# A sparse-attention kernel: GpSimd takes over the test for missed rows and one subtraction, and VectorE's pick moves into its guess update

## The chip, the cores and the metric

The kernel runs on one core of one Trainium2 chip. The metric is the device time of one launch in microseconds. The kernel before took 3318.77 us, the median of 3 runs (3317.39 to 3321.68). Engines are called by the profile's names: PE is TensorE, DVE is VectorE, ACT is ScalarE, POOL is GpSimd, SP is SyncE.

## The reference

The input x is 16 batches of 512 tokens of width 128. One transformer layer is computed on it:

```
x = x + layernorm(attention(layernorm(x)))
x = x + layernorm(ffn(layernorm(x)))

attention, 16 heads of width 64, 16 memory keys in front of the 512 keys:
  dots = (q @ k^T) * scale                     # per head
  dots = einsum('bhij,hk->bkij', dots, pre_proj)   # heads mixed
  dots = where(causal, -max, dots)
  vk   = top_k(dots, 64)[..., -1:]             # the 64th largest of each row
  attn = softmax(where(dots < vk, -max, dots))
  attn = einsum('bhij,hk->bkij', attn, post_proj)
  out  = (attn @ v) @ Wo + bo
ffn: down( silu(gate(x)) * up(x) ), hidden width 384
```

The costly part is the 64th largest of each of 16 x 16 x 512 rows of up to 528 scores.

## The kernel before, in words

**Tiling.** The unit of work is one mixed head of one batch: 512 query rows as four tiles of 128 rows (`t` = 0 to 3), with row lengths 144, 272, 400 and 528 (causal keys and 16 memory keys). There are 16 x 16 = 256 heads, and the program is a software pipeline of steps. Step `s` of batch `b` (`g = 16 b + s`) starts head `g` and works on several older heads at once. Batch 0 (`first`), 14 batches in a loop (`mid`, two a turn), the last batch (`last`) and a `drain` are the same code with different stages left out. Every engine has its own list of instructions, written out by hand; semaphores alone order them against each other, and nothing is reordered.

**Finding the 64th largest.** The kernel guesses a threshold for each row. ACT counts how many scores lie above the guess (the `signs` instructions, three guesses for three heads a step), and DVE moves the guess by a secant step: the *guess update*, eleven small instructions from `miss` to `guesses`, on tiles of 12 or 24 columns (L1113 to L1148). After the third move DVE counts exactly how many scores lie at or above the last guess (`count_found`, L1075, tile `found`) and masks them. POOL subtracts those scores out (L1357, `work`, four instructions a step: the *hide*), and two steps later DVE takes the eight largest of what is left with four MAX8 (L1089). Which of those nine candidates is the 64th is known from `found`. POOL makes rank minus 64 plus `found` for nine ranks (`offset`, L1338), and DVE turns that into zeros and one candidate (L1092) and sums it (L1097): the *pick*, which gives `kth`.

**Missed rows.** Where `found` is too far from the aim, the nine candidates don't hold the 64th. DVE tests that in two small instructions (`spread` L1104 and `missed` L1109). PE adds the marks of all rows up with a tiny matmul into a spare part of a score bank (`raise_flag`, L749), DVE copies the sums out (`flags`, L1072, between two score tiles), reads the total into a register and branches to an exact search (`general_kth`) for the tiles that need it.

**After the threshold.** DVE makes the masked exponentials (`probs`, L1190, four instructions) and their reciprocal sums (`rinv`, L1195). POOL waits for `rinv`, makes four diagonal matrices (`diag`, L1349), and PE uses them to transpose and scale `probs` (L784); ACT copies the result out (L926) and PE multiplies it with the values (L771).

**The order of DVE in a step**: MAX8 x4, pick, miss test, guess update, `count_found` of the two longest tiles, in steps 11 to 13 two products of the FFN (`f_up`, L1164 and L1170) between those two, `probs` x4, `rinv`, `count_found` of the two shorter tiles, then four passes over the new scores in PSUM (L1209) with the flag copy before the last of them. In steps 0, 7, 8 and 14 the statistics of a layer norm follow, in step 10 a maximum over the memory scores.

**The order of POOL in a step**: `negmax` (L1317), seed copy (L1323), memory copy (L1332), `offset` (L1338), in some steps the body of a layer norm (L1258 to L1277), `diag` x4, hide x4, `pmem` (L1363).

## Time and profile before

| | |
|---|---|
| median of the runs | 3318.77 us |
| the profiled execution | 3324.22 us, of which span 3322.4 us |
| mean granted TensorE clock | 0.954 |
| DVE busy | 2884.4 us, 87% |
| ACT busy | 2882.6 us, 87% |
| PE busy | 2794.6 us, 84% |
| POOL busy | 1737.9 us, 52% |
| DMA | mean 7 GB/s |

The span runs from the first to the last instruction of the program. Busy is time in which an engine has an instruction at work; waits, register work and branches of its sequencer are not in it. On DVE a good part of what is not busy lies in gaps of 0.03 to 0.2 us between small instructions that depend on each other. A row of the profile can hide a wait inside an instruction's duration: where an instruction was issued but could not run, its row is longer than that of its fellows.

### The profile page before, as it was taken

What the parts mean: (1) busy time and instruction counts of PE and PEld (TensorE: products, weight loads), DVE (VectorE), ACT (ScalarE), POOL (GpSimd) and SP (SyncE); (2) the same over time, 40 slices, a digit from 0 to 9 for tenths busy, and PEclk for the clock granted to TensorE, in tenths of its full rate; (3) what the DMA queues carried; (4) which work ended last, traced back from release to release, by engine and by line L of the source; (5) the groups of instructions that cost most, each with busy time, mean ns of one, the idle gap of its engine ahead of it and who ended that gap; (6) DMA issues with size and microseconds to landing.
All of it is one profiled execution on the core that took longest, in us unless ns stands there. A gap on an engine that the chain in (4) does not pass through costs nothing. (4 is left out here: it accounts for less than half of the span.)

```text
span 3322.4 us, 76028 instructions
## 1 busy us (share of the span) xinstructions
PE 2794.6 (84%) x16314; PEld 2046.5 (62%) x16314; DVE 2884.4 (87%) x12547; ACT 2882.6 (87%) x8666; POOL 1737.9 (52%) x3623
## 2 busy tenths in 40 slices
PE   6888888888878888888898878888788898888865
PEld 3466666666656666666666656666566666666654
DVE  4599888989989899998889989989889889998884
ACT  1699899998978989899898979989899898989972
POOL 3355555555545555555555545545555555555543
PEclk9999999999989999999999989999999999999987
DMA  1000000000000000000000000000000000000000
GB/s 45 7 2 2 5 8 5 9 2 5 9 5 9 2 12 2 5 9 5 9 2 12 2 5 8 2 12 2 5 9 5 9 2 12 2 5 9 2 8 4
DMA packets 31421, 22.93 MB, mean 7 GB/s; under 512 B 3201, under 2 KB 30338, under 8 KB 30722
## 3 DMA queue, kind: packets, MB, share of 16 engines
q1 hardware_dynamic: 30722, 16.03, 1.7%
q14 instruction: 555, 4.55, 0.5%
q8 instruction: 144, 2.36, 0.3%
HBM read 11.83 MB, written 4.19 MB: 5 GB/s over the span
## 5 line engine op out<-in xcount | busy, mean ns | idle before, releaser
L915 ACT ACTIVATE signs<-scores,state 128x528 int8<-128x528 f32 (+3 forms) x3072 | 1726.3, 585 | 40.5 <-DVE state L1148 40.0
L784 PE MATMUL t_bank<-diag,probs 128*128 128x128 f32 x5120 | 760.9, 308 | 453.8 <-POOL diag L1349 400.5
L1349 POOL TENSOR_SCALAR diag<-ident,rinv 128x128 f32<-128x128 f32 x1024 | 362.2, 374 | 1360.1 <-DVE rinv L1195 1360.1
L784 PEld LDWEIGHTS t_bank<-diag,probs 128*128 128x128 f32 x5120 | 694.2, 216 | 494.1 <-issue 359.1
L1357 POOL TENSOR_TENSOR work<-scores,work 128x528 f32<-128x528 f32 (+3 forms) x1024 | 889.0, 903 | 10.8 <-DVE work L1075 10.8
L760 PE MATMUL s_bank<-xn,gT 128*128 128x512 f32 (+3 forms) x2048 | 685.7, 457 | 0.9 <-ACT gT L846 0.7
L771 PEld LDWEIGHTS y_bank<-u_all,probsT 128*128 128x128 f32 x5120 | 609.0, 192 | 107.3 <-issue 98.9
L915 ACT ACTIVATION_READ_ACCUMULATOR signs<-scores,state 128x1 f32 x3072 | 646.5, 210 | 0.0
L926 ACT COPY probsT<-t_bank 128x512 f32<-128x512 f32 (+1 forms) x768 | 406.9, 530 | 266.3 <-PE t_bank L784 265.1
L771 PE MATMUL y_bank<-u_all,probsT 128*128 128x128 f32 x5120 | 617.3, 276 | 5.3 <-ACT probsT L926 5.3
L1075 DVE TENSOR_SCALAR_CACHE_REDUCE work<-scores,state 128x528 f32<-128x528 f32 (+3 forms) x1024 | 531.1, 553 | 46.2 <-DVE state L1148 46.2
L936 ACT ACTIVATE expo<-scores,negmax 128x528 f32<-128x528 f32 (+3 forms) x1024 | 546.7, 599 | 0.0
L1190 DVE SCALAR_TENSOR_TENSOR probs<-scores,kth,expo 128x528 f32<-128x528 f32 (+3 forms) x1024 | 525.5, 569 | 12.3 <-ACT expo L936 5.8
L1209 DVE TENSOR_SCALAR_CACHE_REDUCE scores<-s_bank,memmax 128x512 f32<-128x512 f32 (+3 forms) x1024 | 516.7, 543 | 6.0 <-PE s_bank L762 6.0
L760 PEld LDWEIGHTS s_bank<-xn,gT 128*128 128x128 f32 x2048 | 326.5, 193 | 227.9 <-issue 220.5
L1089 DVE MAX8 state<-work 128x8 f32<-128x528 f32 (+3 forms) x1024 | 441.6, 491 | 0.2 <-issue 0.2
L632 PE MATMUL misc<-b_all,xn 128*128 128x512 f32 x512 | 273.4, 616 | 7.5 <-ACT u_all L846 7.5
L669 PE MATMUL misc<-xn,a_all 128*128 128x512 f32 x512 | 262.5, 594 | 0.0
L762 PE MATMUL s_bank<-causal,ident 128*128 128x128 bf16 x1024 | 224.6, 219 | 0.0
L762 PEld LDWEIGHTS s_bank<-causal,ident 128*128 128x128 bf16 x1024 | 101.1, 99 | 103.3 <-issue 63.2
L846 ACT COPY u_all<-misc 128x512 f32<-128x512 f32 x256 | 151.4, 591 | 7.0 <-PE misc L632 7.0
L846 ACT COPY gT<-misc 128x512 f32<-128x512 f32 x256 | 154.2, 602 | 0.9 <-PE misc L669 0.9
(156 smaller groups left out, 2846.5 us busy)
## 6 DMA issues: line engine op xcount, KB each, us to landing
xwork<-in_L_attn_x_dram SPq DMA_DIRECT2D x17, 256.0 KB, 2.8
xres<-in_L_attn_x_dram SPq DMA_DIRECT2D x16, 256.0 KB, 2.9
out_dram<-ybuf SPq DMA_DIRECT2D x16, 256.0 KB, 2.4
u_all<-in_L_attn_Wq_dram SPq DMA_DIRECT2D x1, 512.0 KB, 3.6
u_all<-in_L_attn_Wk_dram SPq DMA_DIRECT2D x1, 512.0 KB, 4.5
u_all<-in_L_attn_Wv_dram SPq DMA_DIRECT2D x1, 512.0 KB, 5.5
u_all<-in_L_attn_Wo_dram SPq DMA_DIRECT2D x1, 512.0 KB
expo<-in_L_ffn_w_gate_dram SPq DMA_DIRECT2D x1, 192.0 KB, 4.7
```

Source lines behind the costliest of these rows:

```text
L760: nc.tensor.matmul(score_part(t, 0, KEYS[t]), lhsT=gT[s % 2][:, t * P:(t + 1) * P], rhs=xn[par][:, 0:KEYS[t]], start=True, stop=False, ski ...
L771: mm = nc.tensor.matmul(y_bank[:, t * P:(t + 1) * P], lhsT=probsT[:, h % 2, at:at + P], rhs=u_all[:, j, h * D:(h + 1) * D], start=False, s ...
L784: mm = nc.tensor.matmul(t_bank[q % 2][:, at:at + P], lhsT=probs[:, h % 2, KEY_AT[t] + j * P:KEY_AT[t] + (j + 1) * P], rhs=diag[:, t, :], s ...
L915: nc.scalar.activation(signs[:, k, AT[t]:AT[t] + ROW[t]], row(scores, ring(head_of(s, k + 1), RING), t), ACT.Sign, bias=guesses(s % STATES ...
L926: nc.scalar.copy(probsT[:, h % 2, PART_AT[q]:PART_AT[q + 1]], t_bank[q % 2][:, 0:PART_AT[q + 1] - PART_AT[q]]).then_inc(t_taken, 1)
L936: nc.scalar.activation(row(expo, ring(head_of(s, LAG_E), ERING), t), row(scores, ring(head_of(s, LAG_E), RING), t), ACT.Exp, bias=negmax[: ...
L1075: v.tensor_scalar(work[:, s % 2, AT[t]:AT[t] + ROW[t]], row(scores, slot_k, t), guessed[:, t:t + 1], None, ALU.is_ge, ALU.add, accum_out=f ...
L1089: v.max(candidates(past)[:, t, 1:9], work[:, s % 2, AT[t]:AT[t] + ROW[t]]).then_inc(select_step, 1)
L1190: v.scalar_tensor_tensor(out=probs[:, slot_p % 2, AT[t]:AT[t] + ROW[t]], in0=row(scores, slot_p, t), scalar=kth[:, bass.ds(slot_p, 1), t], ...
L1209: v.tensor_scalar(keys(scores, slot, t), score_part(t, 0, KEYS[t]), 1.0, memmax[par][:, t, bass.ds(s, 1)], ALU.mult, ALU.max, accum_out=ro ...
L1349: nc.gpsimd.tensor_scalar(diag[:, t, :], ident[:, :], rinv[:, slot_p, t:t + 1], 1.0, ALU.mult, ALU.mult).then_inc(scaled, 1)
L1357: nc.gpsimd.tensor_tensor(wrk, row(scores, slot_k, t), wrk, ALU.subtract).then_inc(hidden, 1)
```

## The change

- `offset` is made one step earlier (in the part of the step in which POOL hides, for head `g - 4`), with eleven instead of nine columns and double buffered. The two new columns are `found` minus the two ends of the allowed window.
- `spread` and `missed` move from DVE to POOL: `spread` is the product of the two new columns, `missed` is 1 where it is positive. Both stand on POOL between `diag` and the hide.
- The marks are four columns instead of five; the sum over the tiles is made by DVE's flag copy, which becomes a TENSOR_SCALAR with an accumulated output.
- The subtraction `between` (L1123) moves from DVE to POOL, where it is done for the next step's update as soon as this step's update has ended.
- The pick's first instruction (`weigh_ranks`) stands in front of the last instruction of the guess update, and its second (`pick`) behind it. Before, both stood between MAX8 and the update.
- PE issues `raise_flag` right behind the step's scores, before the values, the weighing and the next G product.
- In steps 11 to 13 the second FFN product stands behind the second `count_found`, no longer directly behind the first product.

```diff
@@ DVE @@
+                    def weigh_ranks():
+                        dve.wait_ge(offset_ready, gp + 1)
+                        dve.wait_ge(select_step, T)
+                        v.scalar_tensor_tensor(out=offset[:, slot_p % 2, :, 2:11], in0=offset[:, slot_p % 2, :, 2:11], scalar=0.0,
+                                               in1=candidates(past), op0=ALU.is_equal,
+                                               op1=ALU.mult).then_inc(select_step, 1)
+                    def pick():
+                        dve.wait_ge(select_step, T + 1)
+                        dve.sem_clear(select_step)
+                        v.tensor_reduce(kth[:, bass.ds(slot_p, 1), :].squeeze(1), offset[:, slot_p % 2, :, 2:12], AX_X,
+                                        ALU.add).then_inc(kth_ready, 1)
...
-                    if checks:
-                        number = found[:, (s - 1) % 2, :]
-                        dve.wait_ge(found_ready, 4 * ge + 4)
-                        alone(dve)
-                        v.scalar_tensor_tensor(out=spread[:, :], in0=number, scalar=-2.0 * AIM, in1=number,
-                                               op0=ALU.add, op1=ALU.mult).then_inc(select_step, 1)
-                        dve.wait_ge(select_step, 1)
-                        at_least(dve, flag_full, ge)
-                        alone(dve)
-                        v.scalar_tensor_tensor(out=missed[:, 0:T], in0=spread[:, :], scalar=WINDOW ** 2 + 0.5 - AIM ** 2,
-                                               in1=active, op0=ALU.is_gt, op1=ALU.mult,
-                                               accum_out=missed[:, T:T + 1]).then_inc(bad_ready, 1)
...
-                        v.tensor_tensor(between[:, :, :], pair(past, S_T, -1), pair(last, S_OTHER, 0),
-                                        ALU.subtract).then_inc(guess_step, 1)
...
+                        dve.wait_ge(between_ready, g - 1)
+                        alone(dve)
...
                         dve.sem_clear(guess_step)
+                        if applies:
+                            weigh_ranks()
                         v.tensor_tensor(guesses(now, 1, GUESSES), guess, move[:, :], ALU.subtract).then_inc(guess_ready, 1)
+
+                    if applies:
+                        if not moves:
+                            weigh_ranks()
+                        pick()
...
-                        v.tensor_copy(flags[:, :], flag_part).then_inc(flag_taken, 1)
+                        v.tensor_scalar(flags[:, 0:T], flag_part, 1.0, None, ALU.mult, ALU.add,
+                                        accum_out=flags[:, T:T + 1]).then_inc(flag_taken, 1)
@@ PE @@
                         score(kind, b, par, s, g)
+                    if lagged(kind, s, LAG_E):
+                        raise_flag(kind, g - LAG_E, head_of(s, LAG_E) % 2)
                     make_extra(kind, b, par, s, 0)
...
-                    if lagged(kind, s, LAG_E):
-                        raise_flag(kind, g - LAG_E)
@@ POOL @@
-                    if lagged(kind, s, LAG_E):
-                        at_least(pool, kth_ready, g - LAG_E)
-                        pool.wait_ge(found_ready, 4 * (g - LAG_E) + 4)
-                        alone(pool)
-                        nc.gpsimd.tensor_tensor(offset[:, :, 0:9], ranks,
-                                                found[:, (s - 1) % 2, :].unsqueeze(2).to_broadcast([P, T, 9]),
-                                                ALU.add).then_inc(offset_ready, 1)
                     extras(kind, b, s)
+                    moves_next = any(lagged(kind, s + 1, k + 2) for k in range(GUESSES)) if s + 1 < H else kind != "drain"
+                    if moves_next:
+                        at_least(pool, guess_ready, g - 1)
+                        at_least(pool, first_ready, g if kind != "drain" or s == 0 else 0)
+                        alone(pool)
+                        nc.gpsimd.tensor_tensor(between[:, :, :], pair((s - 1) % STATES, S_T, -1), pair(s % STATES, S_OTHER, 0),
+                                                ALU.subtract).then_inc(between_ready, 1)
...
                     if lagged(kind, s, LAG_K):
                         gk, slot_k = g - LAG_K, ring(head_of(s, LAG_K), RING)
+                        ranked = offset[:, slot_k % 2, :, :]
+                        at_least(pool, kth_ready, gk - 1)
+                        pool.wait_ge(found_ready, 4 * gk + 4)
+                        alone(pool)
+                        nc.gpsimd.tensor_tensor(ranked[:, :, 0:11], ranks,
+                                                found[:, s % 2, :].unsqueeze(2).to_broadcast([P, T, 11]),
+                                                ALU.add).then_inc(offset_ready, 1)
+                        pool.wait_ge(offset_ready, gk + 1)
+                        alone(pool)
+                        nc.gpsimd.tensor_tensor(spread[:, :], ranked[:, :, 0:1].squeeze(2), ranked[:, :, 1:2].squeeze(2),
+                                                ALU.mult).then_inc(spread_ready, 1)
+                        pool.wait_ge(spread_ready, gk + 1)
+                        at_least(pool, flag_full, gk - 1)
+                        alone(pool)
+                        nc.gpsimd.tensor_scalar(missed[:, slot_k % 2, :], spread[:, :], 0.0, 1.0, ALU.is_gt,
+                                                ALU.mult).then_inc(bad_ready, 1)
```

On DVE, from the last MAX8 of a step in the loop to the first `count_found` of that step, this stood before:

```order
L1089 MAX state<-work 128x8 x2
L1092 SCALAR_TENSOR_TENSOR offset<-offset,state 128x4x9 [waits select_step,offset_ready]
L1096 ISA [waits select_step]
L1097 TENSOR_REDUCE kth<-offset 128x4
L1104 SCALAR_TENSOR_TENSOR spread<-found 128x4 [waits found_ready]
L1109 SCALAR_TENSOR_TENSOR missed<-spread,consts 128x4 [waits select_step,flag_full]
L1122 TENSOR_TENSOR state<-counts,consts 128x12 [waits first_ready,counted2,counted0,counted1]
L1123 TENSOR_TENSOR between<-state 128x24
L1127 TENSOR_TENSOR product<-state 128x24 [waits guess_step]
L1130 SCALAR_TENSOR_TENSOR between<-product,between 128x24 [waits guess_step]
L1134 SCALAR_TENSOR_TENSOR move<-product,state 128x12
```

At the same place DVE has this after the change (first its head, and behind the line of dots its end):

```order
L1107 MAX state<-work 128x8 x2
L1118 TENSOR_TENSOR state<-counts,consts 128x12 [waits first_ready,counted2,counted0,counted1]
L1121 TENSOR_TENSOR product<-state 128x24 [waits guess_step]
L1126 SCALAR_TENSOR_TENSOR between<-product,between 128x24 [waits guess_step,between_ready]
L1130 SCALAR_TENSOR_TENSOR move<-product,state 128x12
...
L1141 TENSOR_TENSOR move<-move,apart 128x12 [waits guess_step]
L1143 ISA [waits guess_step]
L1087 SCALAR_TENSOR_TENSOR offset<-offset,state 128x4x9 [waits select_step,offset_ready]
L1146 TENSOR_TENSOR state<-state,move 128x12
L1093 ISA [waits select_step]
L1094 TENSOR_REDUCE kth<-offset 128x4
```

The guess update now begins directly behind MAX8, and `offset` and `kth` stand around its last instruction; `spread`, `missed` and the first `between` are gone from DVE.

On POOL, a step in the loop from `diag` on, before (`work` is the hide):

```order
L1349 TENSOR_SCALAR diag<-ident,rinv 128x128 x3
L1357 TENSOR_TENSOR work<-scores,work 128x528 [waits found_ready]
L1357 TENSOR_TENSOR work<-scores,work 128x400 [waits found_ready]
L1357 TENSOR_TENSOR work<-scores,work 128x272 [waits found_ready]
L1357 TENSOR_TENSOR work<-scores,work 128x144 [waits found_ready]
L1363 TENSOR_TENSOR pmem<-probs,rinv 128x4x16
L1317 TENSOR_TENSOR negmax<-rowmax,minus_unit 128x4 [waits masked]
L1323 COPY state<-seed 128x2x4 [waits guess_ready]
```

The same step of POOL after the change:

```order
L1354 TENSOR_SCALAR diag<-ident,rinv 128x128 x3
L1362 TENSOR_TENSOR offset<-consts,found 128x4x11 [waits kth_ready,found_ready]
L1367 TENSOR_TENSOR spread<-offset 128x4 [waits offset_ready]
L1372 TENSOR_SCALAR missed<-spread 128x4 [waits spread_ready,flag_full]
L1378 TENSOR_TENSOR work<-scores,work 128x528 [waits found_ready]
L1378 TENSOR_TENSOR work<-scores,work 128x400 [waits found_ready]
L1378 TENSOR_TENSOR work<-scores,work 128x272 [waits found_ready]
L1378 TENSOR_TENSOR work<-scores,work 128x144 [waits found_ready]
```

Three small instructions, two of which wait for the one before, now stand between `diag` and the hide.

## Rows read from the trace of the kernel before

**Rows 1.** Page, part 1: busy time, share of the span, instructions.
```profile
PE 2794.6 (84%) x16314; PEld 2046.5 (62%) x16314; DVE 2884.4 (87%) x12547; ACT 2882.6 (87%) x8666; POOL 1737.9 (52%) x3623
```
**Rows 2.** All `rinv`: count; duration ns min/median/max; first and last start, us.
```profile
L1195 DVE RECIPROCAL rinv<-rowsum x256: 177/178/180, 155.0 to 3278.9; 128x4 f32<-128x4 f32 x128
```
**Rows 3.** Timeline of DVE, step 5 of batch 7: start us, us, engine, line.
```profile
1493.58 0.18 DVE L1195 RECIPROCAL rinv<-rowsum 128x4 f32<-128x4 f32 x1
...
1496.31 1.73 DVE L1089 MAX8 state<-work 128x8 f32<-128x528 f32 x4
1498.15 0.34 DVE L1092 SCALAR_TENSOR_TENSOR offset<-offset,state 128x36 f32<-128x36 f32 x1
...
1498.73 0.16 DVE L1104 SCALAR_TENSOR_TENSOR spread<-found 128x4 f32<-128x4 f32 x1
...
1499.31 0.17 DVE L1122 TENSOR_TENSOR state<-counts,consts 128x12 f32<-128x12 f32 x1
...
1500.68 0.17 DVE L1145 TENSOR_TENSOR move<-move,apart 128x12 f32<-128x12 f32 x1
1500.99 0.17 DVE L1148 TENSOR_TENSOR state<-state,move 128x12 f32<-128x12 f32 x1
1501.33 0.76 DVE L1075 TENSOR_SCALAR_CACHE_REDUCE work<-scores,state 128x528 f32<-128x528 f32 x1 [0.16 <-DVE state L1148]
...
1504.64 0.18 DVE L1195 RECIPROCAL rinv<-rowsum 128x4 f32<-128x4 f32 x1
```
**Rows 4.** Timeline of POOL, the same step.
```profile
1494.01 1.42 POOL L1349 TENSOR_SCALAR diag<-ident,rinv 128x128 f32<-128x128 f32 x4 [5.25 <-DVE rinv L1195]
1495.39 3.47 POOL L1357 TENSOR_TENSOR work<-scores,work 128x528 f32<-128x528 f32 x4
1498.81 0.30 POOL L1363 TENSOR_TENSOR pmem<-probs,rinv 128x64 f32<-128x64 f32 x1
1499.06 0.21 POOL L1317 TENSOR_TENSOR negmax<-rowmax,minus_unit 128x4 f32<-128x4 f32 x1
```
**Rows 5.** POOL's groups by shape: busy us, mean ns of one, idle before.
```profile
L1357 POOL TENSOR_TENSOR work<-scores,work 128x400 f32<-128x400 f32 x256 | 266.2, 1040 | 0.0
L1357 POOL TENSOR_TENSOR work<-scores,work 128x272 f32<-128x272 f32 x256 | 196.5, 767 | 0.0
L1357 POOL TENSOR_TENSOR work<-scores,work 128x144 f32<-128x144 f32 x256 | 127.1, 496 | 0.0
```
**Rows 6.** Timeline of DVE in the drain, where fewer passes precede the update.
```profile
3243.68 0.68 DVE L1104 SCALAR_TENSOR_TENSOR spread<-found 128x4 f32<-128x4 f32 x1
3244.49 0.58 DVE L1109 SCALAR_TENSOR_TENSOR missed<-spread,consts 128x4 f32<-128x4 f32 x1
...
3245.01 0.53 DVE L1122 TENSOR_TENSOR state<-counts,consts 128x12 f32<-128x12 f32 x1
```
**Rows 7.** Timeline of POOL, the same stretch.
```profile
3242.04 3.47 POOL L1357 TENSOR_TENSOR work<-scores,work 128x528 f32<-128x528 f32 x4
```
**Rows 8.** Timeline of POOL, step 9 of batch 7, its layer norm.
```profile
1549.39 0.25 POOL L1258 TENSOR_SCALAR vareps<-meanvar 128x4 f32<-128x4 f32 x1
1549.79 1.04 POOL L1261 TENSOR_TENSOR rstd<-vareps,minus_half 128x4 f32<-128x4 f32 x1
1550.97 1.04 POOL L1270 TENSOR_TENSOR xwork<-xres,rstd 128x512 f32<-128x512 f32 x1
```
**Rows 9.** Timeline of DVE, steps 8 and 9 of batch 7.
```profile
1540.64 1.09 DVE L1190 SCALAR_TENSOR_TENSOR probs<-scores,kth,expo 128x400 f32<-128x400 f32 x1
...
1551.09 0.95 DVE L1148 TENSOR_TENSOR state<-state,move 128x12 f32<-128x12 f32 x1
```
**Rows 10.** DVE's groups that wait: busy us, mean ns | idle before, ended by.
```profile
L1122 DVE TENSOR_TENSOR state<-counts,consts 128x12 f32<-128x12 f32 x258 | 46.0, 178 | 38.0 <-POOL state L1323 8.8 <-ACT signs L915 6.5 <-issue 4.6
L1072 DVE COPY flags<-s_bank 1x5 f32<-1x5 f32 x256 | 37.7, 147 | 20.7 <-issue 20.4
L1170 DVE TENSOR_TENSOR f_up<-f_up,misc 128x512 f32<-128x512 f32 x48 | 33.0, 688 | 10.9 <-DVE f_up L1164 5.9 <-PE misc L728 4.6
```

More of the change, by code:

```diff
@@ L129, in quantile @@
         return low
-    table = np.zeros((P, 2 * T + GUESSES * T + T * 9 + 2 * T), np.float32)
+    table = np.zeros((P, 2 * T + GUESSES * T + T * 11 + T), np.float32)
     for t in range(T):
@@ L139, in guess_table @@
             table[i, T + t] = (z - FAR / (2 * density)) * UNIT ** 0.5
-            table[i, 5 * T + 9 * T + t] = float(active)
-            table[i, 5 * T + 10 * T + t] = 0.0 if active else -FMAX
+            reach = WINDOW + 0.5 if active else FAR
+            table[i, 5 * T + 11 * t] = reach - AIM
+            table[i, 5 * T + 11 * t + 1] = -reach - AIM
+            table[i, 5 * T + 11 * T + t] = 0.0 if active else -FMAX
         for k in range(GUESSES):
             table[:, 2 * T + k * T + t] = ROW[t] - 2 * AIM - 0.25
-        table[:, 5 * T + 9 * t:5 * T + 9 * t + 9] = np.arange(9) - TOPK
+        table[:, 5 * T + 11 * t + 2:5 * T + 11 * t + 11] = np.arange(9) - TOPK
     return table
@@ L343, in build @@
         found = sb("found", [P, 2, T])
-        offset = sb("offset", [P, T, 10])
+        offset = sb("offset", [P, 2, T, 12])
         spread = sb("spread", [P, T])
-        missed = sb("missed", [P, T + 1])
+        missed = sb("missed", [P, 2, T])
         flags = sb("flags", [1, T + 1])
@@ L437, in build @@
         guess_ready = sem("guess_ready")
+        between_ready = sem("between_ready")
         counted = [sem(f"counted{k}") for k in range(GUESSES)]
@@ L444, in build @@
         select_step = sem("select_step")
+        spread_ready = sem("spread_ready")
         bad_ready = sem("bad_ready")
@@ L535, in build @@
         aim_sum = consts[:, 2 * T:5 * T]
[L536 to L537 removed]
+        ranks = consts[:, 5 * T:16 * T].rearrange("p (t n) -> p t n", t=T)
+        cap = consts[:, 16 * T:17 * T]
         ALL = GUESSES * T
@@ L748, in raise_flag @@
                     pe.wait_ge(masked, 4 * H * B)
-                nc.tensor.matmul(flag_part, lhsT=onesP[:, 0:1], rhs=missed[:, :], start=True, stop=True,
+                nc.tensor.matmul(flag_part, lhsT=onesP[:, 0:1], rhs=missed[:, par_e, :], start=True, stop=True,
                                  skip_group_check=True).then_inc(flag_full, 1)
@@ L1055, in _ @@
             dve.wait_ge(state_set, 3)
-            nc.vector.tensor_copy(offset[:, :, 9:10].squeeze(2), cap)
+            nc.vector.tensor_copy(offset[:, :, :, 11:12].squeeze(3), cap.unsqueeze(1).to_broadcast([P, 2, T]))
             def batch(kind, b, par):
@@ L1136, in step @@
                                                in1=miss, op0=ALU.is_gt, op1=ALU.mult).then_inc(guess_step, 1)
-                        dve.wait_ge(guess_step, 4)
+                        dve.wait_ge(guess_step, 3)
                         v.tensor_tensor(other, pair(last, S_OTHER, 0), between[:, :, :], ALU.add).then_inc(guess_step, 1)
+                        dve.wait_ge(guess_step, 5)
+                        v.tensor_tensor(apart[:, :, :], pair(last, S_T, 0), other, ALU.subtract).then_inc(guess_step, 1)
                         dve.wait_ge(guess_step, 6)
-                        v.tensor_tensor(apart[:, :, :], pair(last, S_T, 0), other, ALU.subtract).then_inc(guess_step, 1)
-                        dve.wait_ge(guess_step, 7)
                         v.reciprocal(apart[:, 1, :], apart[:, 1, :]).then_inc(guess_step, 1)
                         v.tensor_tensor(move[:, :], apart[:, 0, :], move[:, :], ALU.mult).then_inc(guess_step, 1)
+                        dve.wait_ge(guess_step, 8)
+                        v.tensor_tensor(move[:, :], move[:, :], apart[:, 1, :], ALU.mult).then_inc(guess_step, 1)
                         dve.wait_ge(guess_step, 9)
-                        v.tensor_tensor(move[:, :], move[:, :], apart[:, 1, :], ALU.mult).then_inc(guess_step, 1)
-                        dve.wait_ge(guess_step, 10)
                         dve.sem_clear(guess_step)
+                        if applies:
+                            weigh_ranks()
                         v.tensor_tensor(guesses(now, 1, GUESSES), guess, move[:, :], ALU.subtract).then_inc(guess_ready, 1)
+                    if applies:
+                        if not moves:
+                            weigh_ranks()
+                        pick()
                     if selects:
@@ L1166, in step @@
                                                ).then_inc(misc_free[gate_at], 1)
+                    if selects:
+                        count_found(ORDER[1])
+                    if 11 <= s < 11 + HC and kind != "first":
                         dve.wait_ge(misc_free[gate_at], turns_of_bank(kind, b, misc_at(kind, ("GATE", c))) + 1)
@@ L1170, in step @@
                         v.tensor_tensor(f_up[:, c, :], f_up[:, c, :], misc[up_at][:, :], ALU.mult).then_inc(misc_free[up_at], 1)
-                    if selects:
-                        count_found(ORDER[1])
                     if applies:
```

21 lines of the change are left out of this document (5 added, 16 removed).

## The prediction, written before the changed kernel was run

> **What bounds the kernel now.** I read the busy table first: DVE and ACT are both at 87%, POOL at 52% [rows 1]. Busy time does not say which of the two sets the pace, so I took the timeline of DVE in a step without extras next [rows 3], from one `rinv` to the next: 1504.64 - 1493.58 = 11.06 us. DVE waits for nobody in it. All that is not busy is gaps of 0.03 to 0.2 us between small dependent instructions. Over the kernel the 256 `rinv` are (3278.9 - 155.0) / 255 = 12.25 us apart [rows 2]; the rest over 11.06 is the steps with layer norm statistics, memory maxima or FFN products. DVE is the bound in all of them. ACT follows, at 2882.6 / 256 = 11.3 us a step at most [rows 1, 2], so a DVE step below about 11.3 us cannot last. What counts is how long DVE takes from `rinv` to `rinv`.
>
> I count a step from its `rinv` (time 0). DVE's MAX8 end at 4.46, `miss` (L1122) starts at 5.73, the update's last small product (L1145) ends at 7.27, the first `count_found` starts at 7.75 [rows 3]. On POOL, which also starts from `rinv`: `diag` at 0.43, hide from 1.81 to 5.28, `pmem` to 5.53, `negmax` to 5.69 [rows 4]. Going back from 5.28 by 0.496 and 0.767, with 0.05 of overlap each, the hide's pieces of 400, 272 and 144 columns end at 4.11, 4.83 and 5.28 [rows 5].
>
> **One rule decides this case, and the trace has it.** In the drain DVE is early against POOL, and its small instructions take 0.68, 0.58 and 0.53 us [rows 6] where they take 0.16 and 0.17 elsewhere [rows 3]. The hide there ends at 3245.51 [rows 7]; with the pieces of rows 5 its inner ends lie at 3244.34, 3245.06 and 3245.51. The three DVE rows end at 3244.36, 3245.07 and 3245.54. So a DVE instruction with two inputs in SBUF that comes while a POOL piece runs ends 0.01 to 0.03 us after that piece, and only one gets through per piece. The layer norms show it too: L1148 takes 0.95 us and ends at 1552.04, POOL's L1270 ends at 1552.01 [rows 8, 9]; `probs` of 400 columns takes 1.09 beside the residual add [rows 9]. In the plain step of before almost none of it is seen, since the hide ends at 5.28 and the update begins at 5.73: only L1092 is stretched, to 0.34.
>
> The Trainium skill speaks against the change here: "GPSIMD Engine Reference", section Key points, says that GpSimd shares its SBUF interfaces with VectorE and contends with DVE instructions that have two SBUF inputs. The trace agrees where POOL streams many columns (0.53 to 0.68 us for 0.16) but not for `rstd` (L1261, 1.04 us, two inputs, 4 columns), beside which DVE's small rows keep their length. By the page alone no size follows; by the trace it is the rest of the running piece.
>
> **The change, part by part.**
>
> *What DVE loses.* `miss` no longer waits behind the pick and the test. It can start at 4.45 in place of 5.73, 1.28 us earlier. The first `between` hid behind `miss`'s latency and gives nothing. Its result now needs a second wait in front of L1126: +0.1, since 0.14 us lie between L1145's end and L1148 [rows 3], behind a clear and a wait, and 0.04 between the small rows that wait once. Behind L1141 stand `weigh`, the last subtraction, a semaphore clear, the reduction and the waits of `count_found`. Before, 0.48 us lay between L1145's end and `count_found`. The same stretch I put at 0.80: 0.21 until `weigh`, 0.15 until the subtraction, 0.21 until the reduction (it waits for `weigh`), 0.23 until `count_found`. So +0.32, and unstalled the step is 1.28 - 0.1 - 0.32 = 0.86 us shorter.
>
> *What POOL gains.* `offset`, `spread` and `missed` stand ahead of the hide: 0.27 + 0.21 + 0.24 us (as `offset` before by width, `negmax` [rows 4] and `vareps` [rows 8]), and two gaps of 0.15 as between `vareps` and `rstd` [rows 8], less 0.05 overlap: the hide starts 0.95 us later, at 2.76. POOL's own idle time (5.25 us a step [rows 4]) takes that at no cost. Its pieces now end at 5.06, 5.78 and 6.23, `pmem` at 6.48, `negmax` at 6.64.
>
> *Together, plain step.* The update that starts at 4.45 runs into all of these. `miss` ends at 5.09 behind the 400 piece, `product` at 5.81 behind the 272 piece, `between` at 6.26, `move` at 6.51 behind `pmem`, `other` at 6.67. From `apart` on it is free (0.67 us to L1145's end before, the same now; up to 0.08 more if the memory copy holds too): 7.38 to 7.46, and `count_found` starts at 8.2, against 7.75. The plain step is 0.43 to 0.51 longer. I take 0.5. The two ends of the unknown are -0.86 (no stall) and +0.5, and I stay at the end that the drain's rows show. There are nine plain steps a batch. At the loop's edges and in some others register work stands ahead of `miss` (part of the 38.0 us of idle time there [rows 10]), which the stall will hide; so for all nine together I put +3.4 us rather than +4.5, an estimate.
>
> *Steps with statistics (1, 8, 9, 15).* The update comes 1.3 us later and meets only the last piece, `pmem` and `negmax`: about 0.3 of stall, a net gain near 0.4. In step 9 the stall of L1148 (0.78) goes, since the update ends before L1270 starts: -1.1. In step 1 a second norm instruction now meets `probs`: -0.35. In steps 8 and 15 both residual adds meet `probs`: 15 gets 0.25 longer. Step 8 gains the flag wait, 20.4 / 16 = 1.3 us [rows 10], since PE makes the marks a whole stage earlier: -1.0. Sum -2.2.
>
> *FFN steps (11, 12, 13).* The second product no longer waits for the first: 10.9 / 48 = 0.23 [rows 10] and some issue time, 0.35 each. Step 11 has the memory maximum ahead and gains 0.4 more. Sum -0.85.
>
> *The flag copy* with its accumulator read costs 0.02. PE's and ACT's lists carry the same work.
>
> *Sum.* +3.4 - 2.2 - 0.85 = +0.35, with the copies +0.7 us a batch. Over 16 batches that is +6 to +11 us, on 3324.22 us of the profiled execution. The median lies 5.5 us below that. With a few starved instructions (an instruction that lost its turn at more than one piece) I say 3330 us.
>
> **The rivals.**
>
> *The stall is smaller* (pieces end earlier, or two DVE instructions pass per piece). Each 0.1 us on the twelve steps concerned is 16 x 1.2 = 19 us. At half the stall, 0.65 us of about 1.3, it is -120 us; a third of that is more likely: 3250 to 3310. For it: the gaps I used are from a few rows. Against it: three drain rows in a line.
>
> *No stall, the full saving.* 0.86 x 256 = 220 us, cut by ACT's 11.3 us a step to some 150: 3170 us. For it: the change takes three instructions off the bound. Against it: rows 6 and 9.
>
> *Slower on the far side.* DVE, kept off for one piece more than its turn, in every second step: +0.5 (a 144 piece [rows 5]) x 128 = 64 us, 3390 us. It decides if POOL's back to back pieces don't give way.
>
> *The miss test late on POOL.* PE's marks need `missed` at 2.8 us of the step before; PE issues them some 7 us after that `rinv`, so no wait. If it did wait, PE's values and weighing would queue behind it, and a step would grow by 1 us. I give it almost nothing.
>
> **How the numbers follow.** The forecast (3315 to 3345) has 0.45, the smaller stall 0.30, the full saving 0.08, the far side 0.17 with the late test. A change under 0.2% (6.6 us) can't be told from none here. Over 3325.4 lie most of the forecast (0.32) and the far side: 0.47 with rounding. Within 6.6 us: 0.17, from the forecast's lower part and the upper edge of the smaller stall. Faster: 0.36. The range 3235 to 3375 leaves out the full saving and half of the far side.
>
> **What would show it.** Right: in a plain step `miss`, `product`, `between` and `move` (L1118 to L1130) take 0.3 to 0.7 us each and end with the hide's pieces and `pmem`; the hide starts 2.7 to 2.8 us after `rinv`; the plain `rinv` distance is 11.5; the flag copy has no idle time before it. Wrong: these four keep 0.17 us, or the hide starts before 2.4 us; then the step falls to ACT's 11.3 or below. If ACT shows no idle time in any step, it has become the bound, and the forecast fails by that.

## The result: slower by 1.8%, in the direction of the forecast but by 60 us instead of 11

| | before | after |
|---|---|---|
| median of the runs | 3320.1 us | 3379.8 us |
| span of the profiled execution | 3322.4 us | 3379.0 us |
| granted TensorE clock | 0.954 | 0.950 |

The ratio is 1.0179, with the 95% interval 1.0163 to 1.0195. The forecast was 3330 us with a range up to 3375; the time lies 5 us above that range.

### The profile page after: what moved, and what is told of

The parts are those of the page before. It is cut to its first block and busy times, and to the rows that moved or that the text cites. A ratio compares the mean times of both kernels' runs of the same rounds, so it can differ in the third digit from the quotient of the medians.

```text
span 3379.0 us, 76754 instructions
## 1 busy us (share of the span) xinstructions
PE 2824.0 (84%) x16314; PEld 2052.9 (61%) x16314; DVE 3024.9 (90%) x11777; ACT 2887.8 (85%) x8666; POOL 1940.8 (57%) x4393
## 5 line engine op out<-in xcount | busy, mean ns | idle before, releaser
L788 PE MATMUL t_bank<-diag,probs 128*128 128x128 f32 x5120 | 748.5, 308 | 478.9 <-POOL diag L1354 467.5
L919 ACT ACTIVATION_READ_ACCUMULATOR signs<-scores,state 128x1 f32 x3072 | 622.3, 203 | 0.0
L1195 DVE SCALAR_TENSOR_TENSOR probs<-scores,kth,expo 128x528 f32<-128x528 f32 (+3 forms) x1024 | 554.9, 597 | 41.1 <-issue 31.7
L636 PE MATMUL misc<-b_all,xn 128*128 128x512 f32 x512 | 284.9, 639 | 9.1 <-ACT u_all L850 9.1
L1345 POOL TENSOR_TENSOR between<-state 128x24 f32<-128x24 f32 x258 | 74.2, 288 | 265.2 <-DVE state L1146 265.2
L1121 DVE TENSOR_TENSOR product<-state 128x24 f32<-128x24 f32 x258 | 157.0, 609 | 9.1 <-DVE state L1118 0.2
```

Source lines behind the costliest of these rows:

```text
L788: mm = nc.tensor.matmul(t_bank[q % 2][:, at:at + P], lhsT=probs[:, h % 2, KEY_AT[t] + j * P:KEY_AT[t] + (j + 1) * P], rhs=diag[:, t, :], s ...
L919: nc.scalar.activation(signs[:, k, AT[t]:AT[t] + ROW[t]], row(scores, ring(head_of(s, k + 1), RING), t), ACT.Sign, bias=guesses(s % STATES ...
L1195: v.scalar_tensor_tensor(out=probs[:, slot_p % 2, AT[t]:AT[t] + ROW[t]], in0=row(scores, slot_p, t), scalar=kth[:, bass.ds(slot_p, 1), t], ...
```

## The profile after

Part 1 of the page, which answers to [rows 1]: DVE has 770 instructions fewer and is busy 140 us longer.

```profile
PE 2824.0 (84%) x16314; PEld 2052.9 (61%) x16314; DVE 3024.9 (90%) x11777; ACT 2887.8 (85%) x8666; POOL 1940.8 (57%) x4393
```

The timeline of DVE in step 5 of batch 7 (start us, us, engine, line), which answers to [rows 3]:

```profile
1522.40 0.18 DVE L1200 RECIPROCAL rinv<-rowsum 128x4 f32<-128x4 f32 x1
...
1525.14 1.73 DVE L1107 MAX8 state<-work 128x8 f32<-128x528 f32 x4
1526.80 0.74 DVE L1118 TENSOR_TENSOR state<-counts,consts 128x12 f32<-128x12 f32 x1
1527.57 0.70 DVE L1121 TENSOR_TENSOR product<-state 128x24 f32<-128x24 f32 x1
1528.41 0.31 DVE L1126 SCALAR_TENSOR_TENSOR between<-product,between 128x24 f32<-128x24 f32 x1
1528.64 0.32 DVE L1130 SCALAR_TENSOR_TENSOR move<-product,state 128x12 f32<-128x12 f32 x1
1528.88 0.24 DVE L1134 TENSOR_TENSOR state<-state,between 128x24 f32<-128x24 f32 x1
1529.16 0.28 DVE L1136 TENSOR_TENSOR apart<-state 128x24 f32<-128x24 f32 x1
...
1530.73 0.76 DVE L1080 TENSOR_SCALAR_CACHE_REDUCE work<-scores,state 128x528 f32<-128x528 f32 x1
...
1534.04 0.18 DVE L1200 RECIPROCAL rinv<-rowsum 128x4 f32<-128x4 f32 x1
```

POOL in the same step, which answers to [rows 4]:

```profile
1525.21 3.47 POOL L1378 TENSOR_TENSOR work<-scores,work 128x528 f32<-128x528 f32 x4
1528.64 0.28 POOL L1384 TENSOR_TENSOR pmem<-probs,rinv 128x64 f32<-128x64 f32 x1
1528.90 0.19 POOL L1322 TENSOR_TENSOR negmax<-rowmax,minus_unit 128x4 f32<-128x4 f32 x1
1529.03 0.18 POOL L1328 COPY state<-seed 128x8 f32<-128x8 f32 x1
1529.17 0.23 POOL L1337 COPY scores<-smem 128x64 f32<-128x64 f32 x1
```

The hide starts 2.81 us after `rinv` and ends at 1528.68; with the pieces of [rows 5] its last three ends lie at 1527.51, 1528.23 and 1528.68. `miss` ends at 1527.54, `product` at 1528.27, `between` at 1528.72, `move` at 1528.96 behind `pmem` (1528.92), `other` at 1529.12 behind `negmax` (1529.09). Each of these five DVE instructions ends 0.03 to 0.04 us after a POOL one, and in this step one gets through per piece. Over the whole kernel `miss` and `product` never take over 0.94 us, so neither loses a second long piece. (The ends inside the hide are worked out from the mean lengths of [rows 5].) The step is 11.64 us; 11.5 was forecast. The groups say it for the whole kernel (busy us, mean ns | idle time before, and what ended it):

```profile
L1121 DVE TENSOR_TENSOR product<-state 128x24 f32<-128x24 f32 x258 | 157.0, 609 | 9.1 <-DVE state L1118 0.2
L1118 DVE TENSOR_TENSOR state<-counts,consts 128x12 f32<-128x12 f32 x258 | 149.8, 580 | 11.1 <-ACT signs L919 7.6 <-issue 3.5
L1076 DVE TENSOR_SCALAR_CACHE_REDUCE flags<-s_bank 1x4 f32<-1x4 f32 x256 | 37.1, 145 | 0.0
L1195 DVE SCALAR_TENSOR_TENSOR probs<-scores,kth,expo 128x528 f32<-128x528 f32 (+3 forms) x1024 | 554.9, 597 | 41.1 <-issue 31.7 <-ACT expo L940 6.0 <-DVE kth L1054 0.7
```

The flag copy waits for nothing, where it had 20.7 us [rows 10]. The last row is new: 31.7 us in which `probs` waits for "issue", that is for nothing but DVE's own sequencer; in the kernel before it was 5.6 us, in 3 waits. No term of the sum has it. The waits give the count, and the timeline one case (step 9 of batch 7):

```profile
DVE probs L1195 <- issue: 31.7, 43, 3.5
```
```profile
1582.06 0.77 DVE L1195 SCALAR_TENSOR_TENSOR probs<-scores,kth,expo 128x528 f32<-128x528 f32 x1 [0.82 <-issue]
```

`probs` stands behind the branch that jumps over the exact search. In the trace's sequencer records the next event mostly comes 0.4 to 0.7 us after that branch. In the kernel before none of 251 such jumps takes 1 to 2 us, and three, near the end of the run, take 2.8 to 2.9 us. The kernel after has those three as well (2.7 to 2.8 us), and besides them 26 that take 1.3 to 1.8 us, all but one at the same steps: 4, 15, 23 and 25 of 32, counted as the head's number modulo 32, since the loop's turn has 32 steps. At step 16 the next event comes after 0.4 us, but `probs` starts only 1.65 to 1.84 us after the branch, where it takes 0.73 us in the kernel before.

## The experiments

All ratios are to the kernel before, run on the same chip.

**Is it the port?** *late_test* is the kernel after with POOL's three new instructions behind the hide.

```diff
 @@ POOL @@
+    for p, t in enumerate(ORDER):          # the hide, four instructions
+        ... tensor_tensor(wrk, row(scores, slot_k, t), wrk, ALU.subtract)
     ... offset, spread, missed ...
-    for p, t in enumerate(ORDER):
-        ... tensor_tensor(wrk, row(scores, slot_k, t), wrk, ALU.subtract)
```

> The changed kernel with POOL's three new small instructions (offset, spread, missed) moved behind the hide, in front of pmem; nothing else differs, and DVE's instructions are the same. Theory (DVE's two-input instructions wait out the piece of the hide that runs): the hide starts at 1.8 us after rinv again, its pieces end at 4.1, 4.85 and 5.3, so miss ends at about 4.85 and product at 5.3, and the first count_found starts near 7.6 in place of 8.33 in a plain step. DVE then comes below ACT's 11.3 us a step in the plain steps, so not all of it shows: 3240 to 3300 us. Rival (the loss of the change is DVE's own: longer tail behind the update and stalls of its sequencer): 3370 to 3390 us, since DVE's program is the same.

Measured: 3212.9 us, ratio 0.968 [0.9664, 0.9696]. DVE and POOL in the same step 5:

```profile
1448.40 1.73 DVE L1107 MAX8 state<-work 128x8 f32<-128x528 f32 x4
1450.06 0.46 DVE L1118 TENSOR_TENSOR state<-counts,consts 128x12 f32<-128x12 f32 x1
1450.55 0.43 DVE L1121 TENSOR_TENSOR product<-state 128x24 f32<-128x24 f32 x1
1451.12 0.18 DVE L1126 SCALAR_TENSOR_TENSOR between<-product,between 128x24 f32<-128x24 f32 x1
```
```profile
1447.47 3.46 POOL L1362 TENSOR_TENSOR work<-scores,work 128x528 f32<-128x528 f32 x4
1450.90 0.25 POOL L1367 TENSOR_TENSOR offset<-consts,found 128x44 f32<-128x44 f32 x1
```

The hide ends at 1450.93, and only `miss` and `product` (to 1450.98) meet it. The plain step falls from 11.64 to 10.74 us. The same work in another order on an engine that is idle 39% of the time is worth 167 us, more than the theory allowed (3240 to 3300). It had taken ACT's 11.3 us a step as a floor for the plain steps. They run at 10.74 us all the same; the mean of all steps is 11.81 us here, so ACT has the longer steps to catch up in. The slow branches are still there (39.9 us of idle time by issue before `probs`), so they are no part of this gain.

*hide_later* is the kernel before with four small POOL instructions (1.0 us) put in front of the hide.

```diff
+    for i in range(4):
+        nc.gpsimd.tensor_tensor(filler[:, i, 1, :], filler[:, i, 0, :], filler[:, i, 0, :], ALU.mult).then_inc(filled, 1)
     for p, t in enumerate(ORDER):          # the hide
```

> The kernel before with four small two-input instructions on POOL (64 columns, on a tile that nobody reads) in front of the hide, and nothing else; this delays the hide by about 1.0 us and leaves DVE's program as it was. Theory: pieces end at 5.1, 5.85 and 6.3, the pick's first instruction, spread, missed and miss are held one piece each, count_found starts 0.7 to 0.85 us later in plain steps, 3430 to 3480 us. Rival (POOL's work off the critical path is free, at 52% busy): 3315 to 3325 us.

Measured: 3497.2 us, ratio 1.0523 [1.0505, 1.054]. In step 5 of batch 7 the old order's small instructions take the stall now:

```profile
1590.11 0.62 DVE L1094 SCALAR_TENSOR_TENSOR offset<-offset,state 128x36 f32<-128x36 f32 x1
...
1590.98 0.41 DVE L1106 SCALAR_TENSOR_TENSOR spread<-found 128x4 f32<-128x4 f32 x1
...
1591.52 0.31 DVE L1111 SCALAR_TENSOR_TENSOR missed<-spread,consts 128x4 f32<-128x4 f32 x1
...
1591.80 0.30 DVE L1124 TENSOR_TENSOR state<-counts,consts 128x12 f32<-128x12 f32 x1
```

This step grows from 11.06 to 11.78 us, within what the theory says. Many others grow more, and that is why the time lies above the expected 3480. In step 5 of batch 8 the pick's first instruction takes 2.08 us:

```profile
1794.94 2.08 DVE L1094 SCALAR_TENSOR_TENSOR offset<-offset,state 128x36 f32<-128x36 f32 x1
```
```profile
1793.18 3.48 POOL L1363 TENSOR_TENSOR work<-scores,work 128x528 f32<-128x528 f32 x4
1796.61 0.30 POOL L1369 TENSOR_TENSOR pmem<-probs,rinv 128x64 f32<-128x64 f32 x1
```

It starts while the piece of 400 columns runs and ends at 1797.02, behind that piece, the two after it (to 1796.66) and `pmem` (to 1796.91). So "one DVE instruction per piece" doesn't always hold: this one lost its turn three times. It takes over 2.0 us in 73 of 256 steps of this execution and 0.96 us at most in the others, and a plain step with it takes 12.79 us in the median where one without takes 11.84. What decides it, the runs don't show. The profiled execution is also the longest of five (3534.7 us; the others 3489 to 3499), so the count of 73 holds for it alone. Nothing was added to DVE, and its busy time grew by 244 us: delaying the hide by 1.0 us is enough to cost 5% in the old order as well.

**Is it the branch?** *before_nobranch* and *after_nobranch* leave out the branch, the register load and the exact search.

```diff
-    rows_missed = dve.value_load(flags[0:1, T:T + 1].bitcast(I32), ...)
...
-    with dve.If(rows_missed > 0):
-        ... general_kth(slot_p, t)
```

> The kernel before without the read of the missed rows' total and without the branch to the exact search (rows that were missed keep the pick's value). Both theories: the four exact searches and their waits go, 4 times some 14 to 16 us, and no sequencer stall of size stood at the branch: 3250 to 3270 us. It is the base for the next kernel.

> The changed kernel without the read of the total and without the branch to the exact search (missed rows keep the pick's value). Theory (of the 57 us by which the profiled spans differ, some 30 to 40 are idle time of DVE's sequencer behind that branch and in front of the pick, at a few fixed places of the loop; the port costs the rest): the distance to the kernel before without the branch shrinks from 57 to 20 to 35 us. Rival (the port costs all of it): the distance stays at 50 to 60 us.

Measured: 3261.0 us (0.9816 [0.98, 0.9832]) and 3276.7 us (0.9871 [0.9854, 0.9887]). Of the 60 us between the kernels 16 are left, fewer than the 20 to 35 that I expected.

*before_short*, *after_short* and *late_short* keep load and branch, and leave out only the body of the search, so that the branch's target lies right behind it. In the traces a search of one tile is 29 records of DVE, so about 116 instructions are no longer jumped over.

```diff
     with dve.If(rows_missed > 0):
-        for t in range(T): ... general_kth(slot_p, t)
```

> The kernel after, with the branch kept and the body of the exact search behind it replaced by one nop, so that the branch's target lies directly behind the branch; the exact search is left out. Theory FETCH (the branch costs 1.3 to 1.8 us at 27 places since the instructions at its target, several hundred bytes to some kilobytes ahead, are not there yet): the idle time of the sequencer in front of probs L1195 (31.7 us by issue) and of L1087 goes, no branch takes over 1 us, and the time comes near that of the kernel without the branch: 3285 to 3330. Rival BRANCH (what costs is the register load and the branch themselves, at places set by what else runs): the slow places stay, time within 0.3% of the kernel after, 3370 to 3385.

> The kernel before with the same edit (exact search left out, branch kept). FETCH: before has hardly any slow branch to lose, so it gains only what the shorter code saves elsewhere: 3285 to 3320; the distance to the short kernel after is 0.3 to 1.3% instead of 1.8%. BRANCH: 3310 to 3325, and the distance stays 1.8%.

> The kernel with the rank and test instructions of POOL behind the hide (3212.9 us), and the exact search replaced by one nop. FETCH: it loses the same slow branches, 3160 to 3195 unless ACT becomes the bound first, which was near at no idle time in some plain steps. BRANCH: 3205 to 3220.

| | us | ratio, interval | instruction packets, queue 14 |
|---|---|---|---|
| before_short | 3275.1 | 0.9859 [0.9844, 0.9874] | 323 (before 555) |
| after_short | 3280.9 | 0.9879 [0.9864, 0.9894] | 342 (after 574) |
| late_short | 3119.6 | 0.9391 [0.9378, 0.9403] | 342 |

```profile
q14 instruction: 574, 4.70, 0.5%
```
```profile
q14 instruction: 342, 2.80, 0.3%
```
```profile
L1191 DVE SCALAR_TENSOR_TENSOR probs<-scores,kth,expo 128x528 f32<-128x528 f32 (+3 forms) x1024 | 560.0, 602 | 8.0 <-ACT expo L940 6.6 <-issue 1.0
```

The first line is of the kernel after (number, MB), the other two of after_short. No branch of it takes over 1 us, and the idle time of `probs` by issue falls from 31.7 to 1.0 us. The kernels now lie 5.7 us apart. Both lose the four exact searches that a run makes: 57.2 us in the kernel after, 56.3 before (the steps with a search, long against short). Outside these four steps the kernel after loses 48.8 us more by being cut, the kernel before none (it is 5.5 us longer). So of the 57.0 us by which the stretch from the first to the last `rinv` grew, 55 go with the jump and 1.8 are left.

That 1.8 is flattered by its base. In before_short step 15 takes 13.9 us in nine of 14 batches, where it takes 13.0 in before_nobranch: the statistics wait for ACT there (8.0 us in 10 waits for `ybuf` L901, against 3.5 in one) and the flag copies wait in 28 steps instead of 19. Outside the searches the kernel after loses 49.8 us in it, about as much as above, the kernel before 7.5, and 14.2 of the 57.0 us are left. So the two pairs agree on what the jump costs in the kernel after (49 to 50 us), and leave 2 to 14 us to everything that the prediction counted, 6 to 16 by the medians.

All three short kernels came in below their expected times (3285 to 3330, 3285 to 3320, 3160 to 3195); I had forgotten the searches, some 56 us in each. In late_short ACT is 92% busy (2867.6 of 3117.6 us) and DVE 90%; the plain step is 10.74 us as in late_test. That ACT would be the next bound is not shown.

Of the 48.8 us, 26.0 lie in the 26 steps with a slow branch and 10.7 in the eight steps 16; the rest is spread over many steps, and I have no row for it.

**Why one kernel and not the other?** *after_pre20* puts 20 instructions (two fulfilled waits each) once in front of DVE's loop. Nothing else changes. (The theories COUNT and, in the runs with nops below, PACKET say that only the number of DVE instructions in a step counts, since it sets how far an instruction packet is ahead of the branch. CROWDING says that more work for DVE's sequencer near the branch only costs.)

```diff
+            for _ in range(40):
+                dve.wait_ge(table_in, 16)
             batches(dve, batch)
```

> The kernel after with 20 instructions (each two waits that have long been fulfilled) put once ahead of VectorE's loop over the batches; nothing in the loop changes but that its code starts 20 instructions later. (The nops of the earlier kernels left no instruction in the program, whose trace has the same 17972 records for VectorE, so those runs only repeated the kernels.) Theory PLACE (whether an instruction packet starts just ahead of a branch depends on where the code lies): the slow steps 4, 15, 16, 23, 25 of a turn become others, and the time goes to anything from 3325 to 3400. Rival COUNT (it depends only on how many instructions lie between one branch and the next): the same steps are slow, 3375 to 3385.

Measured: 3344.7 us, ratio 1.0077 [1.006, 1.0094]: twenty instructions *more*, 35 us *less*. The slow branches move to steps 1 and 8, all but one of them, and are 16 instead of 26.

```profile
DVE probs L1195 <- issue: 17.4, 19, 3.5
```

The trace records each 8 KB packet of instructions with its start, and it shows what a slow branch waits for (us from the branch; worked out from the trace's records, a few cases of each; the sums of the others are 1.79 to 2.03):

```
kernel, step of turn      last packet before branch   branch to next event   sum
after, 4                  -0.46                       1.35                   1.81
after, 15                 -0.46                       1.36                   1.82
after, 23                 -0.44                       1.37                   1.81
after, 25                 -0.18                       1.62                   1.80
after_pre20, 1            -0.42                       1.39                   1.81
after_pre20, 8            -0.11                       1.71                   1.82
```

DVE goes on 1.8 us after the start of that packet: the median is 1.81 in the kernel after (26 branches, one of them with no packet ahead of it) and 1.81 in after_pre20 (16). The branches of 2.8 us that both kernels have fit as well: there a packet starts 1.0 us behind the branch, at g = 240, and the next event comes 1.8 us after it. In step 16 a packet starts 0.06 to 0.08 us ahead of the branch, and `probs` comes 1.72 to 1.91 us after it (seven of the eight; the eighth is the one at g = 240).

So DVE waits for a packet that is in flight, or is only asked for, as the branch is taken. That it waits because its target or what stands right behind it is in that packet is the reading that fits all of these; the trace doesn't say what a packet holds. A packet near a branch is not enough by itself: in after_short 24 branches have one up to 1.0 us ahead, in before_short 16, and none of them takes over 0.5 us. There the target lies right behind the branch. Packets of other engines come in the same queue, and in the kernel after 19 of the 225 others have one within 1.1 us too. A packet that starts 1.2 us ahead is there in time, which is how the kernel before has it (step 4: packet at -1.18, next event after 0.66).

The Trainium skill, "Runtime: NRT & Kernel Launch", section Instruction fetch mechanics, says that a taken branch whose target isn't in the window of two pages must wait until the page has been fetched. That DVE waits at such a branch agrees with the trace; that the window decides it, no run here shows. The trace gives the size: 1.8 us from the packet's start, less what the packet is ahead.

*late_wait4* is late_test with four such instructions in every step, ahead of the branch, which gives DVE as many records as in the kernel before (18996 in the run, 1024 more than in late_test).

```diff
                     if applies:
+                        for _ in range(8):
+                            dve.wait_ge(table_in, 16)
                         at_least(dve, t_full, 3 * (gp - 1))
```

> The kernel with POOL's ranks and test behind the hide (3212.9 us) with 4 such instructions in every step, behind the second count_found and ahead of the waits before the branch. A step then has as many instructions on VectorE as in the kernel before (190 from branch to branch, with the jumped-over search, instead of 186). PLACE and COUNT both let the slow branches go or become few: 3160 to 3190, and the fastest complete kernel. CROWDING (only the sequencer's work counts): 3215 to 3230, same slow steps.

Measured: 3254.9 us, ratio 0.9804 [0.9788, 0.9821], 42 us slower than late_test. The slow branches became few and shorter (9 of 1.0 to 1.5 us, at other steps, for 28 of over 1.3 us), but the plain step went from 10.74 to 11.04: the branch now stands 0.40 us later behind `count_found`, and `probs` starts 0.32 us later. Four fulfilled waits ahead of a branch cost 0.3 us, or 0.3 x 256 = 77 us, more than the cure gave. The expectation (3160 to 3190) missed that price.

**A rival that the rows rule out.** The mean granted TensorE clock differs from run to run, from 0.914 in hide_later over 0.950 in the kernel after to 0.988 in late_short, and so does PE's pace. But DVE's waits for PE come to 17 to 26 us in each of these kernels (22 before, 17 after, 21 in hide_later, 26 in late_short), so PE's pace can make up a few us of these differences and no more.

**Runs that only repeat.** *after_pad16*, *after_pad40*, *before_pad16* (nops ahead of the loop), *after_skip32* (nops in the search) and *after_nop4*, *after_nop8*, *before_nop8*, *late_nop8* (nops ahead of the branch) were meant to move code or to add sequencer work.

```diff
+            for _ in range(16):
+                dve.nop(nofuse=True)
             batches(dve, batch)
```

> The changed kernel with 16 instructions without effect on DVE ahead of the first batch, once; everything behind them lies 16 instructions further on in DVE's program. Theory (the idle time behind the branch to the exact search, at steps 4, 15, 16, 23 and 25 of the 32 of a loop turn, is fetching of DVE's instructions, and depends on where they lie): other steps have it, and the median moves by up to 40 us either way. Rival (it comes from the data flow at those steps): the same steps have it, 3375 to 3385 us.

> The same with 8 nops. PACKET: all of the six places are free, about 3325 to 3345 (the 52 us of stalls less what 8 nops cost). CROWDING: 3385 to 3420. If the places where a packet meets the branch only move on to others, the time stays at 3370 to 3390 with new slow places.

These nops left no instruction in the program: DVE's records number 17972 in the kernel after and in all its variants with nops, 18996 in the kernel before and its two, and the instruction packets are the same 574 and 555. So the times (3377.1, 3375.0, 3378.5, 3378.9 and 3378.3 us for the kernel after, 3319.3 and 3322.5 for before, 3214.2 for late_test) say nothing of either theory. They show how well a time repeats, within 0.15%, with the same slow steps each time. The first three looked like a refutation of the theory that the place of the code counts; they were none, and after_pre20 bears it out.

**One part alone.** *raise_early* is the kernel before with PE's `raise_flag` right behind the scores.

```diff
                         score(kind, b, par, s, g)
+                    if lagged(kind, s, LAG_E):
+                        raise_flag(kind, g - LAG_E)
...
-                    if lagged(kind, s, LAG_E):
-                        raise_flag(kind, g - LAG_E)
```

> The kernel before with PE's raise_flag moved directly behind the step's scores, as in the changed kernel; nothing else. Theory: the wait of the flag copy in step 7 (20.4 us in all) goes, and some of it comes back as a later wait: 3300 to 3312 us. Rival (that wait is not PE's but the fetch of DVE's instructions): 3317 to 3323 us.

Measured: 3299.4 us, ratio 0.9945 [0.9931, 0.9958]. That is 18.7 us less, of the 20.4 that the flag copy had waited, just below the 3300 to 3312 expected. Its flag copy has no idle time left:

```profile
L1072 DVE COPY flags<-s_bank 1x5 f32<-1x5 f32 x256 | 37.7, 147 | 0.0
```

## Why the prediction was wrong in size

**The step that failed is the sum itself: it has no term for DVE's own instruction supply.** I read from [rows 3] that DVE waits for nobody and took every gap as belonging to dependences of small instructions. The branch stood in the code and, as a cost, in no row. In the kernel before it cost next to nothing, its 0.6 us being covered by `count_found`. The change took four instructions from each step, the packets came to stand elsewhere against the branches, and with the jump the kernel after loses 49 to 50 us that it doesn't lose without. 3330 and these 50 make the 3380 measured; that is worked out afterwards, and no row of the kernel before would have given it.

**Point by point**, us per batch of the loop:

| steps | forecast | after - before | after_short - before_short | after_nobranch - before_nobranch |
|---|---|---|---|---|
| nine plain | +3.4 | +5.8 | +4.6 | +4.0 |
| with statistics (1, 8, 9, 15) | -2.2 | -2.8 | -4.3 | -3.4 |
| FFN (11 to 13) | -0.85 | +0.4 | -0.7 | -0.1 |
| sum | +0.35 | +3.4 | -0.5 | +0.5 |

With the jump cut, the forecast sum and the two measured ones agree within a microsecond a batch, and the medians differ by 5.7 and 15.7 us where I had put +6 to +11. Part of that agreement is luck, since errors cancel in it. The plain steps cost more than I took, since I granted them 1.1 us of cover at the loop's edges that isn't there, and the memory copy (L1337, in the plain step to 1529.40) does hold `apart` (0.28 for 0.18 us, end 1529.44). The steps with statistics gained 1.2 to 2.1 us more than I gave them: step 8 goes from 14.66 to 12.90 in the short pair, -1.8 for -1.0, and step 15 got no longer, where I had put +0.25. And the FFN term doesn't follow from its own parts: three times 0.35 and 0.4 are 1.45, and with the stall of 0.5 in each of the three steps, which the first rival counts on twelve steps, 0.05 are left and not 0.85.

**Right:** the port rule and its numbers. The hide at 2.76 (measured 2.81), `count_found` at 8.2 (8.33), the four update instructions at 0.3 to 0.7 us each with the pieces of the hide (0.74, 0.70, 0.31, 0.32), the plain step at 11.5 (11.64), the flag wait gone. ACT was not the bound. That a DVE step below 11.3 us "cannot last" was wrong for a plain step, as the 10.74 us of late_test show. "Only one gets through per piece" holds in the kernel after, and one in four picks of hide_later shows that none may get through for several pieces. **The rivals:** the smaller stall and the full saving did not come, as all of these rows show. "Slower on the far side" gave 3390 and the time came near it, by another mechanism: in the kernel after neither `miss` nor `product` is kept off for a second long piece. Close to the number is not right. Its mechanism exists, though: in hide_later the pick is kept off so in 73 steps.

**Open:** what sets the place of a packet, and when DVE loses its turn at more than one POOL instruction. Adding 20 instructions moved it, and taking four from each step did; the address at which one falls I could not derive. That late_test with some instructions ahead of its loop would lose its slow branches too was not run; it is the fastest complete kernel here, at 3212.9 us.

## What to carry to other kernels

When work is moved to an engine with idle time, ask beside what it will run there before asking what it costs: with three small instructions in front of POOL's hide this change costs 1.8%, with the same three behind it it gains 3.2%. And where an engine's program jumps over a large block in each step, count "idle by issue" as a cost that any edit to its list can bring or take; a time that moves by 1% between two edits of one loop may be this alone, and a few instructions ahead of the loop tell it, provided that they are in the program: nops were not, waits long fulfilled were. Base such a judgement on two different ways to take the block out, since a base can have waits of its own, as before_short has.

## What the runs showed of the hardware

- A DVE instruction with two inputs in SBUF that meets a running POOL instruction ends 0.02 to 0.04 us after it, whatever its own size (0.17 becomes up to 0.74 us behind one piece of the hide); the pick's `offset` ends about 0.08 us or more after it. Behind POOL's hide, `pmem` and `negmax` this was one DVE instruction per POOL instruction in the kernel after, and `apart` was held by a copy with one input. In hide_later DVE's `offset` was kept off by four POOL instructions in a row, 2.0 to 2.2 us, in 73 of 256 steps. Beside `rstd` (1.04 us, two inputs of 4 columns) DVE's small instructions keep their 0.16 to 0.23 us.
- A jump over the exact search costs 0.6 to 0.7 us from branch to next event, with its target right behind it 0.4 us. Where a packet of instructions has started shortly before it (or starts 1.0 us behind it), DVE goes on 1.8 us after that packet's start.
- The code jumped over is fetched, or nearly all of it: 232 packets more in either kernel, for 256 jumps, which is 7.4 KB for each. By the 66 bytes that before_short moves for each record of the engines other than PE (323 packets of 8 KB, 40098 records), an estimate, that is 112 instructions, and the search is about 116.
- Four more instructions of DVE's sequencer, each two waits long fulfilled, cost 0.3 us a step just ahead of a branch, though DVE's engine was at work on 528 and 400 columns when they were reached.
- The exact search for one step costs 10 to 16 us, four times in a run.
